# One-core transformer kernel: the first attention phase's stacks built by TensorE from the split parts, with ropes, parts and projections interleaved

## What is computed

```
x = layernorm(x)
q, k, v = x @ W                       # heads of 16 channels
q, k = rope(q), rope(k)               # A and C
y = softmax(q @ k.T / 4, masked) @ v
x = x_in + y @ Wo
```

## Time and profile before

| | us |
|---|---|
| median of 3 runs (lowest, highest) | 2077.81 (2076.68, 2078.71) |
| profiled execution: its own time | 2074.05 |
| profiled execution: span, first to last instruction | 2072.3 |
| PE busy | 1865.8 (90%) |
| DVE busy | 1055.4 (51%) |
| ACT busy | 904.7 (44%) |
| POOL busy | 676.2 (33%) |
| mean granted PE clock | 0.93 |

### The profile page before, as it was taken

How to read it: one execution, slowest core, us unless ns; L and a number is a source line. 1 busy time by engine, 2 the same in 40 slices (tenths; PEclk the granted TensorE clock), 3 DMA queues, 4 the chain that set the end, 5 groups by cost and what they waited for, 6 DMA issues and landing times. The chain is left out here.

```text
span 2072.3 us, 30156 instructions
## 1 busy us (share of the span) xinstructions
PE 1865.8 (90%) x10530; PEld 1274.0 (61%) x10537; DVE 1055.4 (51%) x1790; ACT 904.7 (44%) x1897; POOL 676.2 (33%) x571
## 2 busy tenths in 40 slices
PE   5899899999997898899999994999985879999997
PEld 3333688888885455788878862233254457777775
DVE  4765344444444554444444452888534345555533
ACT  3577333333334564333333332588831135555521
POOL 4100366666662102556666624100000142323200
PEclk7799899999998899999999997799987579999998
DMA  4300344444421401544444404700005000000000
GB/s 124 91 1 1 93 118 106 106 114 117 115 64 36 105 1 42 132 114 116 114 109 110 117 0 102 88 1 1 1 1 118 1 1 1 1 2 1 1 1 21
DMA packets 139430, 123.86 MB, mean 60 GB/s; under 512 B 84769, under 2 KB 125241, under 8 KB 139161
## 3 DMA queue, kind: packets, MB, share of 16 engines
q1 hardware_dynamic: 139321, 122.41, 23.9%
HBM read 113.57 MB, written 8.65 MB: 59 GB/s over the span
## 5 line engine op out<-in xcount | busy, mean ns | idle before, releaser
L1205 DVE TENSOR_TENSOR e_inner_lo<-e_inner,e_inner_hi 128x512 fp32r<-128x512 f32 x192 | 245.5, 1278 | 402.3 <-ACT e_inner_hi L1174 402.1
L1193 POOL TENSOR_TENSOR e_wsilu<-e_silu,e_rw 128x512 f32<-128x512 f32 x192 | 261.6, 1363 | 235.3 <-ACT e_silu L1168 172.7
L1144 PE MATMUL psum<-e_x_hi,e_w_hi 128*128 128x512 f32 x768 | 305.7, 398 | 6.6 <-DVE e_inner L1213 6.4
L1144 PE MATMUL psum<-e_x_lo,e_w_hi 128*128 128x512 f32 x768 | 301.4, 392 | 0.0
L1144 PE MATMUL psum<-e_x_hi,e_w_lo 128*128 128x512 f32 x768 | 301.0, 392 | 0.0
L1168 ACT ACTIVATE e_silu<-psum 128x512 f32<-128x512 f32 x192 | 114.8, 598 | 358.4 <-PE psum L1144 358.2
L1200 POOL TENSOR_TENSOR e_w_lo<-e_raw,e_w_hi 128x384 fp32r<-128x384 f32 x180 | 221.0, 1228 | 129.7 <-ACT e_w_hi L1181 116.4
L901 DVE TENSOR_REDUCE c_mx<-psum 128x1 f32<-128x1024 f32 x128 | 151.3, 1220 | 53.5 <-PE psum L777 53.5
L1144 PEld LDWEIGHTS psum<-e_x_hi,e_w_hi 128*128 128x128 f32 x768 | 145.8, 190 | 48.6 <-DVE e_inner L1213 17.2
L1159 PE MATMUL psum<-e_inner_hi,e_w_hi 128*128 128x512 f32 x384 | 152.1, 396 | 15.2 <-DVE e_inner_lo L1205 13.2
L1144 PEld LDWEIGHTS psum<-e_x_hi,e_w_lo 128*128 128x128 f32 x768 | 145.6, 190 | 31.2
(11 more groups left out here) (327 smaller groups left out, 3220.7 us busy)
## 6 DMA issues: line engine op xcount, KB each, us to landing
e_rw<-e_rw_dram SPq DMA_DIRECT2D x60, 384.0 KB, 5.2
e_rw<-e_rw_dram SPq DMA_DIRECT2D x60, 256.0 KB, 5.4
e_raw<-in_L_ffn_w_gate SPq DMA_DIRECT2D x64, 192.0 KB, 2.6
e_raw<-in_L_ffn_w_up SPq DMA_DIRECT2D x64, 192.0 KB, 2.5
e_raw<-in_L_ffn_w_down SPq DMA_DIRECT2D x32, 384.0 KB, 3.6
e_rw<-e_rw_dram SPq DMA_DIRECT2D x68, 128.0 KB, 4.9
a_qs<-a_parts_dram SPq DMA_DIRECT2D x48, 64.0 KB, 2.2
b_qs<-b_parts_dram SPq DMA_DIRECT2D x48, 64.0 KB, 2.3
```

The lines of the kernel that those rows point to most:

```text
L1144: last = nc.tensor.matmul(bank[u % 2][:], self.w[a][s][:, KC * which + k, j * P:(j + 1) * P], self.x[b][:, k, h * HALF:(h + 1) * HALF], st ...
L1193: self.core.nc.gpsimd.tensor_tensor(self.wsilu[:, u % 2, :], self.silu[:, u % 2, :], self.rw[s][:, j, h * HALF:(h + 1) * HALF], ALU.mult). ...
L1205: self.core.nc.vector.tensor_tensor(self.inner_parts[1][:, u % 3, :], self.inner[:, u % 2, :], self.inner_parts[0][:, u % 3, :], ALU.subtr ...
```

## The change

The stacks of phase 0 are no longer read back from memory. For A and B these are 4 query heads of half 0 and key head 0 of half 0 (5 stacks of 96 x 512); for C 4 query heads of half 0 and 4 key heads of both halves (12 stacks). A new class `MadeStacks` makes each one by three bf16 matmuls, one for each part, with a selection matrix of zeros and ones as weights (`pick`, made by POOL: 2 memsets and 12 small copies, once each for A, B and C), into bank 6 or 7; ACT copies the even ones and DVE the odd ones to `qs` / `ks`. The other stacks still go through memory, by the same code, and each (half, group) has its own semaphore.

Around that, work moves:

- A: DVE takes rests 0 and 1 before rope 4, rest 2 before rope 6, and copies stacks 1 and 3 before rope 6. POOL takes third parts 0 and 1 before rope 7. Units 3 to 5 and the 11 raw transposes move between the first maxima (before maxima 2, 3, 7 and 9 to 14).
- B: tiles 6 and 7 are projected before maxima 0 and 2, units 3 to 5 are turned before maxima 4, 5, 9; the DVE rests go before maxima 7, 8, 12. ACT takes the second root earlier, and the turn of the second half of the input comes before units 0 and 1.
- C: the projection gives q and k only (2 x 512 columns a tile); v is projected in the next block, one tile before each of maxima 2 to 9, into banks 4 to 6, with ACT copying. Turns come between projections 5 to 7. DVE does ropes 0 and 2 before its store of xT, and takes the odd third parts from POOL. Unit 5 and unit 4 of C swap places. The 6 query DMAs of (half 1, group 0) move behind the barrier, before the 72.

The core of the diff:

```diff
     def project(self, pe, t):
...
-        wide = cfg.width > HALF
-        slots = 2 if wide else 4
...
+        n = min(HALF, cfg.width)
+        for k in range(KC):
+            last = nc.tensor.matmul(core.bank[self.PROJECTED[t]][:, 0:n], core.xT[:, k, t * P:(t + 1) * P],
+                                    self.w[:, k, 0:n], start=(k == 0), stop=(k == KC - 1))
         last.then_inc(self.projected, 1)
+    PROJECTED = (0, 1, 2, 3, 0, 2, 1, 3)
...
+    def project_values(self, pe, t, projected, copied):
...
+        for k in range(KC):
+            last = nc.tensor.matmul(core.bank[4 + t % 3][:, 0:D], core.xT[:, k, t * P:(t + 1) * P],
+                                    self.w[:, k, HALF:HALF + D], start=(k == 0), stop=(k == KC - 1))
...
+class MadeStacks:
...
+    def pick(self, pool, r):
+        for kind in ("q", "k"):
+            nc.gpsimd.memset(self.picks[kind][:], 0.0).then_inc(self.picked, 1)
...
+        for s, parts in enumerate(PAIRS):
+            for kind, a in zip(("q", "k"), parts):
+                nc.gpsimd.tensor_copy(self.picks[kind][:, a, :, s * HD:(s + 1) * HD], heads).then_inc(self.picked, 1)
...
+    def make(self, pe, proj, n):
...
+        pe.wait_ge(proj.part1, unit + 1)
+        pe.wait_ge(proj.part2, unit + 1)
+        proj.wait_part3(pe, unit)
+        if n >= 2:
+            pe.wait_ge(self.copied[n % 2], self.done(r, n % 2) + n // 2)
+        for a in range(PARTS):
+            last = nc.tensor.matmul(core.bank[6 + n % 2][0:ROWS, :], self.picks[kind][0:rows, a, x, :],
+                                    proj.part[h][0:rows, a, j, :], start=a == 0, stop=a == PARTS - 1)
+        last.then_inc(self.ready, 1)
...
@@ A on PE
-        for n in range(len(self.a.units)):
+        for n in range(3):
             self.a.turn(pe, n)
-        pe.wait_ge(self.a.v_copied, TT)
-        for i in range(len(start.raw)):
-            start.turn(pe, i)
...
+        for n in range(5):
+            self.made.make(pe, self.a, n)
+        def ahead(what, p, *more):
+            if what == "max" and p == 0:
+                n = QUART * more[0] + more[1]
+                if n in (2, 3):
+                    self.a.turn(pe, n + 1)
+                if n == 7:
+                    self.a.turn(pe, 5)
+                for i in range(len(start.raw)):
+                    if n == 9 + i // 2:
+                        start.turn(pe, i)
...
@@ C on PE, on DVE
+        for t, n in ((4, None), (5, 0), (6, 1), (7, 2), (None, 3)):
+            if t is not None:
+                c.project(pe, t)
+            if n is not None:
+                c.turn(pe, n)
+        for n in range(4):
+            self.made.make(pe, c, n)
+        c.turn(pe, 4)
+        for n in range(4, 8):
+            self.made.make(pe, c, n)
+        for n in range(5, 8):
+            c.turn(pe, n)
+        for n in range(8, 12):
+            self.made.make(pe, c, n)
...
+        for t in (0, 2):
+            c.rotate(dve, nc.vector, 0, t)
         norm.store_vector(dve, 4, 1, 1, (6, 7))
+        c.rotate(dve, nc.vector, 0, 4)
+        c.take_rest(dve, 0)
+        c.take_rest(dve, 1)
+        c.rotate(dve, nc.vector, 0, 6)
+        c.take_part3(dve, nc.vector, 1)
+        c.take_rest(dve, 2)
+        c.take_rest(dve, 3)
+        c.take_part3(dve, nc.vector, 3)
+        for n in (1, 3):
+            self.made.copy(dve, nc.vector.tensor_copy, c, n)
...
@@ third_attention
+            def ahead(what, p, *more):
+                if what == "max" and p == 0 and 2 <= QUART * more[0] + more[1] < 2 + TT:
+                    c.project_values(pe, QUART * more[0] + more[1] - 2, projected, copied)
+                if what == "rows" and (p, *more) == (0, 0):
+                    pe.wait_ge(copied, TT)
```

More of the change, by code:

```diff
@@ L489, in project @@
             pe.wait_ge(self.w_loaded, 16 * self.n_loads)
-        wide = cfg.width > HALF
-        slots = 2 if wide else 4
[L492 to L499, removed]
+        if t >= 4:
+            pe.wait_ge(self.copied, t - 3 + (t == 5))
+            if self.tag != "c":
+                pe.wait_ge(self.v_copied, t - 3 + (t == 5))
@@ L935, in vector @@
         for what, *args in self.order:
+            ahead(what, *args)
             if what == "max":
@@ L2369, in vector, with ahead @@
+        for n in (1, 3):
+            self.made.copy(dve, nc.vector.tensor_copy, a, n)
+        a.rotate(dve, nc.vector, 0, 6)
+        def ahead(what, p, *more):
+            if what == "max" and p == 0:
+                n = QUART * more[0] + more[1]
+                if n in (5, 6):
+                    a.take_rest(dve, n - 2)
+                if n == 10:
+                    a.take_rest(dve, 5)
+        self.layer_of_vector(dve, 0, ahead)
         self.norm_behind_experts(dve, 0)
-        self.b.take_rest(dve, 0)
@@ L2371, in vector, with ahead @@
         norm.store_vector(dve, 2, 1, 1, (6, 7))
-        for n in range(1, len(self.b.units)):
-            self.b.take_rest(dve, n)
-        self.layer_of_vector(dve, 1)
+        for n in range(3):
+            b.take_rest(dve, n)
+        for n in (1, 3):
+            self.made.copy(dve, nc.vector.tensor_copy, b, n)
+        def ahead(what, p, *more):
+            if what == "max" and p == 0:
+                n = QUART * more[0] + more[1]
+                if n in (7, 8):
+                    b.take_rest(dve, n - 4)
+                if n == 12:
+                    b.take_rest(dve, 5)
@@ L2506, in _ @@
         def _(sp):
-            for g in range(1, 4):
+            for g in range(4):
                 for h in range(2):
@@ L2518, in _, with ahead @@
         def _(pe):
-            attend.tensor(pe, c.wait_stacked, nothing)
+            def ahead(what, p, *more):
+                if what == "max" and p == 0 and 2 <= QUART * more[0] + more[1] < 2 + TT:
+                    c.project_values(pe, QUART * more[0] + more[1] - 2, projected, copied)
+                if what == "rows" and (p, *more) == (0, 0):
+                    pe.wait_ge(copied, TT)
+            attend.tensor(pe, c.wait_stacked, nothing, ahead)
         @block.scalar
         def _(act):
+            for t in range(TT):
+                c.copy_values(act, t, projected, copied)
             attend.scalar(act, nothing)
```

363 lines of the change are left out of this document (241 added, 122 removed).

## The result

| | before | after |
|---|---|---|
| median (lowest, highest), 4 runs each, us | 2077.24 (2075.73, 2078.71) | 2051.37 (2050.28, 2052.22) |
| profiled execution: own time / span, us | 2074.05 / 2072.3 | 2051.34 / 2049.6 |
| mean granted PE clock | 0.93 | 0.946 |

The ratio of after to before is 0.9875, with a 95% interval of 0.9858 to 0.9892: 26 us faster. Forecast 2054, range 2046 to 2067. The total was right, and so was the mechanism. The shares of the three attentions were not, and the clock gave its part at other places than forecast.

What follows compares the result with a forecast made beforehand. PE's waits for stacks from memory before the first maxima (37.9 us together) and a PE-led chain were taken as the bound. Terms -5.7 (A), -3.7 (B), -11.0 (C), -3.3 (clock) sum to -23.7: median 2054, range 2046 to 2067 us.

Steps and rivals of the forecast that it cites:

- A, first maximum 13.0 earlier: Attention A: with stacks made on PE, DVE's first maximum comes near 35.5 us instead of 48.5.
- A, given back 7.3: Attention A: turns, rests, raw transposes and picks no longer hidden under the wait cost +7.3, leaving first shift -5.7 us.
- B, first maximum -6.9, shift -3.7: Attention B: first maximum at 667.8 instead of 674.7; work between the maxima costs +3.2, leaving first shift -3.7 us.
- C, first maximum -13.0, shift -11.0: Attention C: first maximum at 1280.3 instead of 1293.3; v tiles between the maxima cost +2.0, leaving -11.0 us.
- v's +2.0: Attention C: v tiles between the maxima begin at half clock, then run at full, costing +2.0 us over eight tiles.
- make 0 at 1255.0, make 3 ready at 1260.7: Attention C, walk of makes, copies and splits: first stack made at 1255.0, stack 3 ready at 1260.7.
- The clock, -3.3: Behind the maxima, PE keeps full clock: B gains 1.8, C 1.5, A nothing; -3.3 us, bounds 0 and -10.
- (a): Rival: full clock throughout, lifted by A's raw transposes too; -30.4, 2047 us; chance 17%.
- (b): Rival: v tiles in C run at half clock, costing 11.0 instead of 2.0; -13.2, 2065 us; chance 13%.
- (c): Rival: phase 2's stacks arrive late in A and B, which then give nothing; -12.5, 2065 us; chance 12%.
- (d): Rival: make and copy in lock step at half clock, in all three attentions; +10, 2088 us; chance 5%.
- (e): Rival: the change does nothing; phase 0's maxima are made earlier but the order is held elsewhere; 2078 us; chance 3%.

Runs made afterwards that it cites:

- all_memory: Changed kernel with its new order kept, but all phase-0 stacks fetched from memory again; 2069.24 us, ratio 0.9971 to the kernel before.
- Experiment 10: Changed kernel with C's first two made-stack copies placed earlier in the ACT and DVE lists; 2046.02 us, ratio 0.9853 to the kernel before.
- c_copies: Changed kernel with C's first made-stack copy earlier on ACT and its second earlier on DVE; 2046.02 us, ratio 0.9853 to the kernel before.
- combined: Changed kernel with A's raw transposes spread one per maximum and C's first two copies earlier; 2046.36 us, ratio 0.9869 to the kernel before.

## Why the prediction was right, step by step

**A, first maximum 13.0 earlier:** 12.4 (36.09 against 48.47). The chain of rests, third parts and makes went as walked, one us late: first make at 29.2 instead of 28.1 (the projection itself ended 1.0 later; the first norm was slower beside POOL's picks, where one small DVE instruction took 0.82 instead of 0.17, and for the picks 0.5 had been taken, among the terms given back), and rope 4 beside POOL cost 3.26 (27.53 to 30.79) against 3.2 priced. The Trainium skill, SBUF — State Buffer, section SBUF: two separate sides, says that a DVE instruction with two SBUF inputs and a GpSimd instruction that reads SBUF exclude each other. The 1.33 against 0.49 us of one rope instruction agree.

**A, given back 7.3:** 6.0 (36.09 to 50.60, less the 8.5 before). The transposes bound PE as forecast; a wait of 1.77 for ACT's copy of an earlier one was not foreseen. Of the 1.3 less than forecast 0.5 are the picks', which cost before the first maximum; the rest is not divided among the terms. Shift **-5.7**: -6.4, and -6.0 on average at the second shift. Right.

**B, first maximum -6.9, shift -3.7:** from the start of its projection to DVE's first maximum B took 27.1 and 27.6 before, and after it 17.6, or 19.6 where the projection was at low clock as in before: 7.5 to 8.0 like for like, against 6.9 forecast, so that term held within 1. From the end of project 5 (653.5) to the maximum it took 7.3, the forecast's walk had 7.5 (660.3 to 667.8). Between the maxima the forecast has +3.2, and it was 1.3 (9.72 against 8.45). This is not because the added work was cheaper. The granted clock was another one: the lines are the whole stretch and then two pairs of maxima on DVE, before, and the same after.

```profile
674.70:683.60 8.90, 8.01 (x42) 2.71 (x42) 6.16 (x17) 0.00 (x0) 0.00 (x0) 0.50 0.54 155
...
680.35 0.88 DVE L901 TENSOR_REDUCE b_mx<-psum 128x1 f32<-128x260 f32 x2 [0.28 <-PE psum L783]
681.50 0.88 DVE L901 TENSOR_REDUCE b_mx<-psum 128x1 f32<-128x260 f32 x2 [0.28 <-PE psum L783]
```

```profile
660.50:670.50 10.00, 7.99 (x59) 4.33 (x57) 7.21 (x19) 4.58 (x10) 3.29 (x3) 0.96 0.42 132
...
666.50 0.74 DVE L1005 TENSOR_REDUCE b_mx<-psum 128x1 f32<-128x260 f32 x2
667.43 0.76 DVE L1005 TENSOR_REDUCE b_mx<-psum 128x1 f32<-128x260 f32 x2 [0.18 <-PE psum L885]
```

A pair of maxima comes every 1.15 us at 0.50 and, where nothing stands between, every 0.93 at 0.96. Over the six to eight pairs of the phase that is 1.3 to 1.8, an estimate, so the added work cost 2.6 to 3.1, near the 3.2. The clock was 0.91 and 1.00 in the two later executions of after and 0.98 in all_memory; no run has the new order at half clock here, so the split is not shown by an experiment. The projection's clock (7.34 to 5.40 in the profiled pair, 7.2 to 6.1 on average) came on top, an accident. B's whole, -7.7 at the second shift on average, is twice the -3.7.

**C, first maximum -13.0, shift -11.0:** -9.8 and -7.8 against its own entry in the profiled pair, -7.0 at the second shift on average. v's +2.0 was exact there (2.4 in the two later executions), and so was the 6.5 from the last third part to the first maximum (1259.56 + 0.68 to 1266.71). The step that failed is the walk "make 0 at 1255.0, make 3 ready at 1260.7": after make 0 and 1 PE stood 3.65 us, since copy 0 stood behind second parts 2 and 3 on ACT and copy 1 behind third part 3 on DVE, and DVE's two early third parts took 1.20 and 1.15 beside POOL where its last took 0.68. Make 3 was ready 7.9 us after make 0, not 5.7: 2.2 of the 3.2 by which the first maximum was late. Of the rest 0.6 was lost before make 0 and 0.4 behind make 3. Whether DVE pays more by these parts than POOL saves, as the forecast has it, no run shows. The walk had given each engine its work by duration, not by the order of its list. Experiment 10 took 1.6 to 3.6 us back.

**The clock, -3.3:** not where it was put. From first to second shift B took 12.1 before and 12.3 after, C 23.3 and 23.2 (24.2 in the two later executions); the rows of C ran at 0.65. The rows also left less room than the "about 3.0" of the forecast, which took DVE's own work in that stretch for "5 or so": the row has DVE busy for 6.64 of the 8.3, so 1.7 at most. For B's 1.8 no row was shown. What the clock did give lay in B before its first shift: the estimated 1.3 to 1.8 between the maxima and some 1.2 in the projection. Beyond that there is 3.3 less elsewhere on average, within the 5 us by which "elsewhere" differs among three executions of after, so nothing can be claimed for it.

**The sum:** -23.7 forecast, -20.6 in the three parts on average and -22.7 in the profiled pair's spans. B came out 4 better, some 3 of it by a clock that had been put elsewhere; C came out 4 worse, the clock in the rows 3 worse, and elsewhere 3 came by chance. The total fell where it did by these offsets, and not because each term was known to 1 us. On the profiled execution the forecast was 2050.4 against 2051.34; the 2.6 us between 2054 and the median come of the 3.8 by which before's profiled execution lay under its median, which after's (2051.34 and 2051.37) did not.

**Rivals.** (a) fell in A, where the transposes took 1.06 for four matmuls as before; in C the v tiles ran at 0.71 and then 0.87, between (a) and (b), and DVE hid all but 2.0 of them. (c): no PE wait for a DMA at phase 2. (d), slower: its sign, gaps of over 1.5 us between makes, was there twice in C (3.65 and 1.78), so make and copy did fall into lock step in places, but elsewhere two banks and two copiers overlapped: five stacks took 4.9 us in B. (e) fell with the waits.

**What the forecast did not separate** is the stacks from the order. It put all gain down to the missing wait. In B that holds: made stacks are 7.8 of 7.8. In A they are 3.4 of 6.0. In C it mostly does not: made stacks brought the first maximum 1.9 earlier, and the order gives the rest of the 7; with the v tiles bare in front of the maxima all 7 were gone.

## What to carry to other kernels

Before a transfer is replaced by arithmetic, ask what stands behind it: in A and B nothing did, and making the stacks paid 11 us in the ledger; in C a barrier did, and twelve makes brought the first maximum only about 2 us earlier, while moving v under another engine's work paid 7. Read the granted clock of a stretch before a cheaper or dearer stretch is put down to the work in it. Walk a make-and-copy chain by each engine's list, not by sums of durations; a small copy behind two splits cost 3.65 us. Where single executions differ by 5 us, judge an edit of 2 by the stretch it touches in the trace, and say that the median can't show it.

## What was not expected of the hardware

- The same program meets the low clock in other places from one execution to the next: B's projection took 5.40 and 7.37 us in two executions of after. Of the eleven executions with B's new order five had 5.40 and six between 7.08 and 7.60. Over 14 profiled executions the work outside the three attentions took between 1852.6 and 1862.8 us, though but for the picks the kernels are the same there.
- Executions of one kernel spread by 8 to 10 us here (c_copies 2041.42 to 2050.74, combined 2043.86 to 2053.95, before 2071.23 to 2079.16 on one chip). A 95% interval of four or five runs was 0.3 to 0.5% wide, wider than most single edits of this study.
- PE kept busy by v tiles in 1265.6 to 1274 reached full clock in the second tile (tiles of 1.91, 1.32, then 1.03 us). It fell back at 1284, with maxima alone in between, where PE idles about 0.5 us before each, and was 0.65 in the rows.
